# A share of channel 14's exponentials moved from ScalarE to a power on GpSimd

## The reference

```python
for wl in range(16):                       # channels
    m = cos(phase_modulators[wl])          # one number per head
    scores = (Q * m) @ (K * m).T * SCALE
    scores = scores * cos(KERR * scores * scores)
    acc += softmax(scores) @ V * interference_weights[wl]
x = layernorm(x + (acc / 16) @ Wo + bo)
x = layernorm(x + ffn(x))                  # shared FFN, and 8 experts for 256 positions
```

## Time and profile before

| | |
|---|---|
| time, median of 3 runs | 3418.81 us (3414.29 to 3419.89) |
| profiled execution, time | 3416.68 us |
| profiled execution, span | 3414.5 us |
| ACT busy | 3318.0 us |
| DVE busy | 3275.0 us |
| PE busy | 2630.6 us |
| POOL busy | 231.7 us |

### The profile page before, as it was taken

How to read it: one execution, slowest core, us unless ns; L and a number is a source line. 1 busy time by engine, 2 the same in 40 slices (tenths; PEclk the granted TensorE clock), 3 DMA queues, 4 the chain that set the end, 5 groups by cost and what they waited for, 6 DMA issues and landing times.

```text
span 3414.5 us, 47798 instructions
## 1 busy us (share of the span) xinstructions
PE 2630.6 (77%) x20611; PEld 760.9 (22%) x20611; DVE 3275.0 (96%) x3000; ACT 3318.0 (97%) x611; POOL 231.7 (7%) x319
## 2 busy tenths in 40 slices
PE   7778777777777778777778788777887778777765
PEld 2212222212221222222222222222222222222224
DVE  7999999999999999999999999999999999999997
ACT  7999999999999999999999999999999999999992
POOL 0000000000000000000010111110111101111100
PEclk8999999999999999999999999999999999999997
DMA  1000000000000000000000000000000000000001
GB/s 49 1 1 1 1 1 1 1 1 1 1 1 1 1 1 1 1 15 1 1 2 2 4 2 4 2 1 4 2 4 2 4 1 2 4 2 16 2 17 30
DMA packets 20792, 16.04 MB, mean 5 GB/s; under 512 B 4257, under 2 KB 18994, under 8 KB 20338
## 3 DMA queue, kind: packets, MB, share of 16 engines
q1 hardware_dynamic: 19314, 12.28, 1.2%
q10 hardware_dynamic: 1152, 0.53, 0.1%
q0 software_dynamic: 128, 0.26, 0.0%
HBM read 7.70 MB, written 5.37 MB: 4 GB/s over the span
## 4 chain that ended last, share of the span: by engine, by line
issue 49%; DVE 21%; ACT 17%; PE 6%; POOL 5%; ACTq 1%; DMA 0%; POOLq 0%; DVEq 0%
ACT probs L681 17%; PE psum L1371 4%; DVE x_y L752 3%; DVE x_p L768 2%; DVE x_p L760 2%; DVE s_t L909 2%; DVE x_p L764 2%; DVE x_p L772 2%; DVE m_pad L897 1%; ACTq L671 1%; DVE x_2k L749 1%; DVE o_sb L1501 1%; POOL loop_memory L525 1%; POOL loop_memory L530 1%; DVE x_2k L756 1%
## 5 line engine op out<-in xcount | busy, mean ns | idle before, releaser
L681 ACT ACTIVATE probs<-s_t 128x8192 f32<-128x8192 f32 x447 | 3100.8, 7024 | 9.2 <-PE psum L1371 8.3
L1371 PE MATMUL psum<-probs,v_pad 128*27 128x512 f32 x15136 | 1882.0, 637 | 543.8 <-ACT probs L681 507.9
L1371 PEld LDWEIGHTS psum<-probs,v_pad 128*27 128x27 f32 x15136 | 461.0, 112 | 1882.6 <-issue 1023.5
L752 DVE SCALAR_TENSOR_TENSOR x_y<-s_t,c_last,x_2k 128x2048 f32<-128x2048 f32 (+1 forms) x160 | 369.6, 2310 | 2.4
L764 DVE SCALAR_TENSOR_TENSOR x_p<-x_p,x_y 128x2048 f32<-128x2048 f32 (+1 forms) x160 | 358.2, 2239 | 4.4
L772 DVE SCALAR_TENSOR_TENSOR x_p<-x_p,x_2k 128x2048 f32<-128x2048 f32 (+1 forms) x160 | 357.7, 2236 | 3.9
L768 DVE SCALAR_TENSOR_TENSOR x_p<-x_p 128x2048 f32<-128x2048 f32 (+1 forms) x160 | 357.2, 2232 | 2.4
L760 DVE SCALAR_TENSOR_TENSOR x_p<-x_y 128x2048 f32<-128x2048 f32 (+1 forms) x160 | 356.3, 2227 | 0.0
L897 DVE TENSOR_REDUCE m_pad<-psum 128x4 f32<-128x2048 f32 x128 | 292.3, 2285 | 4.1 <-PE psum L831 3.1
L909 DVE COPY s_t<-psum 128x2048 f32<-128x2048 f32 x128 | 291.8, 2281 | 4.4 <-PE psum L871 4.3
L831 PE MATMUL psum<-k_t,q_t 8*128 8x512 f32 x1024 | 161.4, 703 | 103.7 <-DVE m_pad L897 82.5
(11 more groups left out here) (243 smaller groups left out, 1135.8 us busy)
## 6 DMA issues: line engine op xcount, KB each, us to landing
s_t<-in_L_attn_x_dram SPq DMA_DIRECT2D x4, 256.0 KB, 7.3
x_next_dram<-x_p SPq DMA_DIRECT2D x1, 1024.0 KB, 3.8
x_group<-x_next_dram SPq DMA_DIRECT2D x1, 1024.0 KB, 4.9
loop_memory<-in_L_attn_x_dram SPq DMA_DIRECT2D x8, 128.0 KB, 2.1
x_dram<-loop_memory SPq DMA_DIRECT2D x8, 128.0 KB, 1.8
out_dram<-loop_memory SPq DMA_DIRECT2D x8, 128.0 KB, 1.8
x_dram<-probs SPq DMA_DIRECT2D x2, 512.0 KB, 5.1
out_dram<-probs SPq DMA_DIRECT2D x2, 512.0 KB, 3.6
```

Of the source, the lines that this page charges most:

```text
L681: nc.scalar.activation(probs[:, (p + w) % 2, :], s_t[:, p, :], ACT.Exp, scale=scales[(p + w) % 2]).then_inc(s["exp_done"], 1)
L752: nc.vector.scalar_tensor_tensor(out=y, in0=scores, scalar=scale, in1=at, op0=ALU.mult, op1=ALU.subtract) \
L1371: last = nc.tensor.matmul(products_of(u, wg)[L * b:L * b + SLOTS * A, :], v_pad[:, p, b * T + kt, c0:c0 + SLOTS * A], probs[:, (p + w) % 2 ...
```

## The change

In units 0 to 15 the 512 columns of key tile 2 and batch 3 in channel 14 (columns 5632 to 6143) go from ScalarE to GpSimd. GpSimd raises e to c2 once for all heads (`e_last`, 128x16), then per unit raises `e_last` of the head to the score, into a buffer of its own (`x_pow`), and multiplies it by 12068.069. TensorE takes that batch from `x_pow`, as the first of channel 14's matmuls. VectorE's work keeps its place and size.

```diff
-ACT_LAST = [T * X_COLS - (NB - b) * S for b in SHARED_B]
+DVE_LAST = [T * X_COLS - (NB - b) * S for b in SHARED_B]
+POOL_HALF, POOL_KT, POOL_B = 0, T - 2, NB - 1
+ACT_LAST = [n - S * (g == POOL_HALF) for g, n in enumerate(DVE_LAST)]
...
+                nc.gpsimd.tensor_tensor(e_last[:], e_base[:].broadcast_to([P, H]), c2[:, WA - 1, :], ALU.pow).then_inc(s["pow_used"], 1)
+
+                def power(u, p, h):
+
+                    pool.wait_ge(s["pow_used"], u + 1)
+                    n0 = POOL_KT * X_COLS + POOL_B * S
+                    nc.gpsimd.tensor_tensor(x_pow[:], e_last[:, bass.ds(h, 1)].broadcast_to([P, S]), s_t[:, p, n0:n0 + S], ALU.pow) \
+                        .then_inc(s["pow_raised"], 1)
+                    pool.wait_ge(s["pow_raised"], u + 1)
+                    nc.gpsimd.tensor_tensor(x_pow[:], x_pow[:], exp2_one[:].broadcast_to([P, S]), ALU.mult).then_inc(s["pow_ready"], 1)
+
                 def pair_of_units(g, i, last=False):
...
                             stage(i * 2 + half + 1, 1 - half)
+                        if g == POOL_HALF:
+                            power(i * 2 + half, half, i * 2 + half)
...
+                        if g == POOL_HALF and w == WA - 1:
+                            pe.wait_ge(s["pow_ready"], u + 1)
+                            nc.tensor.matmul(products_of(u, wg)[L * POOL_B:L * POOL_B + SLOTS * A, :],
+                                             v_pad[:, p, POOL_B * T + POOL_KT, c0:c0 + SLOTS * A], x_pow[:],
+                                             start=False, stop=False).then_inc(s["pow_used"], 1)
                         for kt in range(T):
                             for b in range(SHARED_B[g] if w == WA - 1 and kt == T - 1 else NB):
+                                if g == POOL_HALF and w == WA - 1 and (kt, b) == (POOL_KT, POOL_B):
+                                    continue
```

More of the change, by code:

```diff
@@ L134, in postln_kernel @@
         x_next = x_p[:, 0, :]
+        x_pow = sb("x_pow", [P, S])
+        e_base = sb("e_base", [P, 1])
+        e_last = sb("e_last", [P, H])
+        exp2_one = sb("exp2_one", [P, 1])
         x_2k = sb("x_2k", [P, X_COLS], BF16)
@@ L260, in products_of @@
             return psum[:, 7, :] if wg == NWG - 1 else o_ps[(v * (NWG - 1) + wg) % 2]
-        names = ("x_loaded_0 x_loaded_1 x_loaded_2 x_loaded_3 x2_loaded w_staged ffw_copied ffw_shifted qk_projected w_summed_copied sw3_zeroed w_loaded ffw_loaded pm_loaded xg_loaded masks_zeroed b_loaded masks_ready xn_stored "
+        names = ("x_loaded_0 x_loaded_1 x_loaded_2 x_loaded_3 x2_loaded w_staged ffw_copied ffw_shifted qk_projected w_summed_copied sw3_zeroed w_loaded ffw_loaded pm_loaded xg_loaded masks_zeroed pow_step pow_raised pow_ready pow_used b_loaded masks_ready xn_stored "
                  "i_loaded i_ready e_loaded e_zeroed ew_turned ew_ready gathered scattered m_pe m_dve m_act "
@@ L557, in _ @@
             with pool.If(fast == 1):
+                nc.gpsimd.memset(exp2_one[:], EXP2_ONE)
+                nc.gpsimd.memset(e_base[:], float(np.e)).then_inc(s["pow_step"], 1)
+                pool.wait_ge(s["c2_step"], 7)
+                pool.wait_ge(s["pow_step"], 1)
+                nc.gpsimd.tensor_tensor(e_last[:], e_base[:].broadcast_to([P, H]), c2[:, WA - 1, :], ALU.pow).then_inc(s["pow_used"], 1)
[6 more added lines that the diff above has]
+                    nc.gpsimd.tensor_tensor(x_pow[:], x_pow[:], exp2_one[:].broadcast_to([P, S]), ALU.mult).then_inc(s["pow_ready"], 1)
                 def pair_of_units(g, i, last=False):
@@ L741, in piece_dve @@
             piece, base = u * PIECES + n, (u * PIECES + n) * PIECE_LINKS
-            w, start, cols = (W - 1, n * X_COLS, X_COLS) if n < T else (WA - 1, ACT_LAST[u // H], T * X_COLS - ACT_LAST[u // H])
+            w, start, cols = (W - 1, n * X_COLS, X_COLS) if n < T else (WA - 1, DVE_LAST[u // H], T * X_COLS - DVE_LAST[u // H])
             scores = s_t[:, p, start:start + cols]
```

## The result

| | before | changed |
|---|---|---|
| time, median | 3418.11 us (20 runs) | 3426.03 us (20 runs) |
| ratio to before, 95% interval | | 1.0024 (1.0017 to 1.0030) |
| profiled execution: time, span | 3416.68, 3414.5 us | 3425.91, 3423.7 us |

The account below looks back on a forecast made before the run. ScalarE was taken as the bound at 102.34 of 102.47 us per unit; with GpSimd's holds VectorE would need 167.6, 65.1 more per unit, 1042 us over 16 units: 4459, forecast as 4460 us, range 3405 to 5560.

Parts of the forecast that it names:

- I expect reading to go on at the pace of the computing, so the hold lasts nearly as long as the power: GpSimd's 512-column power keeps VectorE's two-SBUF-input instructions out for nearly its whole 67 us, 65.1 us more per unit.
- (67 - 0.2) for the power: VectorE's time per unit lost to GpSimd's power: 67 us long, less some 0.2 us of overlap at an end.
- (1.1 - 0.2) for the multiplication: VectorE's time per unit lost to GpSimd's 512-column multiplication: 1.1 us long, less 0.2 us, counted as 0.9.
- VectorE's L1512 in the middle of a two-column power: Contrary row: a two-SBUF-input multiplication ran in 0.17 us, its usual 0.176, so the hold ends once inputs are read.
- The 256-column addition: GpSimd row, 0.59 us from its release, beside which VectorE's L752 lost 0.35 us; taken as whole-instruction exclusion.
- The power's length: GpSimd's 512-column power: 1.6 us if the extra is paid once, 133 if per column; 67 taken.
- Rival 1: GpSimd's hold is short; VectorE loses the multiplication's 0.9 us and something per chunk: 3410, up to 3416 us; chance 0.22.
- within the 2.1: VectorE's spare us per unit after the change: ScalarE's 102.0 against VectorE's 99.9.
- The 2.6 us: VectorE's spare time per unit before the change, taken as 102.47 - 99.89.
- Sixteen units give 7.0 us, all of it on the bound: ScalarE's partial exponential gets 0.44 us shorter in each of 16 units, the whole possible gain, 0.2% of the time.
- where the first hold falls: At a unit's start the power waits for VectorE's L768 to end, then holds L772 behind it.
- TensorE's new wait: TensorE waits for `x_pow` at channel 14; setting the pace only in rival 2, 3969 us, chance 0.09.

## Why the prediction was wrong

- **The step that failed** is "I expect reading to go on at the pace of the computing, so the hold lasts nearly as long as the power". At 512 columns the hold was 0.72 us, not 66.8. The term "(67 - 0.2) for the power" should have been 0.7, the term "(1.1 - 0.2) for the multiplication" was 0.72. With both put right the sum reads 99.9 + 0.7 + 0.7 = 101.3 us of VectorE, under ScalarE's 102.0, and would forecast a gain of 7 us; a loss of 8 was measured, so two further steps below failed as well. The forecast mechanism is real, but it begins above 544 columns. The same sum for 1024 columns, 99.9 + 165.3 - 0.2 = 265.0 us of VectorE per unit, meets the 262.6 us that those units took.
- **The row that told it** was cited and set aside: VectorE's L1512 in the middle of a two-column power. The 256-column addition was given more weight, but an addition that is done in 0.59 us can't part a hold while reading from a hold while running.
- **The power's length** was taken as 67 us within 1.6 to 133; it is 82 without its wait. The sizes 16, 256, 512, 640 and 1024 took 2.94, 43.2, 84.0, 104.4 and 165.3 us, 0.16 us per column; by that, some 0.3 of the two-column row's extra 0.52 us recur and 0.2 are paid once. All but the 16-column one include about 2 us of waiting for VectorE.
- **Rival 1 was right on the hold, wrong on the sum.** It said that 0.9 us for the multiplication and something for the power lie "within the 2.1" that VectorE has to spare. The 2.6 us came from 102.47 minus busy time, and most of that is not spare: it is some 1.5 us between the ends and starts of 79 instructions per unit. Between 145 and 1690 us the kernel before shows VectorE waiting

```profile
DVE r_z L1510 <- PE psum L1341: 16.6, 15, 1.3
```

  1.1 us per unit. Against that stand two holds of 0.72 us. Nor are these waits simply used up first: with 19 us of holds the changed kernel's VectorE still waits

```profile
DVE r_z L1540 <- PE psum L1364: 12.5, 9, 2.7
```

  since the holds lie on the loop, behind the place where it waits.
- **"Sixteen units give 7.0 us, all of it on the bound"** failed too. ScalarE looked as if it had no gap, but its own pace is 102.23 us and a loop over three engines took 102.4. Taking channel 14's columns away with no power leaves units at 102.4; taking them from channel 7 brings 101.9 in the mean. No term of the prediction was for TensorE's clock, which decides how long that loop is.
- **The rule of the Trainium skill** ("SBUF — State Buffer", section "Who interferes with whom"), a lock for the whole instruction, holds for the addition and for VectorE's own operations, and nearly for powers of 640 and 1024 columns, in whose middle one VectorE operation got in. For powers of up to 544 it does not: there the measurement decides, and VectorE with two SBUF inputs ran for 79 us beside a GpSimd instruction that had read from SBUF.
- **Right**: that GpSimd's instructions wait for the end of VectorE's and hold the next one, where the first hold falls, the multiplication's price (0.9 us taken, 0.72 measured), and that TensorE's new wait would not be at fault. That the change loses at all was forecast too, but for a reason that does not hold at this size; the direction was luck, and scaling the values in place of the exponentials was enough to turn it.

## What to carry to other kernels

Work for an idle engine is priced by what it takes from the others while it reads and writes, not by its length: look for a row in which the neighbour runs in its middle, and ask whether the new size still fits what is read at once. Spare time of an engine is at most what its waits say, not span minus busy time. Where two engines look full, check which instructions lie on the loop that closes from unit to unit before shortening one that does not. Look at the units one by one: here four of fifteen carried most of a loss that the mean spreads over all.

## What the runs showed of the hardware

- That the engines wait for one another by semaphores only, as the opening section has it, is not so for GpSimd and VectorE. A GpSimd power of two SBUF operands holds a VectorE instruction with two SBUF inputs by 0.29 us at 256 columns, 0.72 at 512, 0.77 at 544, and for 81 us and more at 640 and 1024.
- VectorE's TENSOR_SCALAR with a single tensor input is held as well: L772 by 0.66 us beside a 512-column multiplication, L770 by 78.5 us in the second part of the 1024-column power. Between the two parts the first held instruction, L793, ran to its end.
- A power begun just as VectorE copies from PSUM to SBUF for 2.28 us cost it nothing, fourteen times out of fourteen.
- 40 matmuls of TensorE took 4.7, 6.4 and 8.0 us at a mean granted clock of 1.00, 0.74 and 0.58.
- GpSimd computes a power at 0.16 us per column of 128 partitions, 70 times the 2.3 ns per column of the addition (0.59 us for 256).
